# A recurrent layer's input projection, moved from a stage of its own into the steps of the recurrence

## The chip, the core and the metric

One NeuronCore of a Trainium2 chip runs the whole kernel. The metric is device time in microseconds (us); lower is better. The engines are named as in the profile: PE is TensorE (PEld its weight loads), DVE is VectorE, ACT is ScalarE, POOL is GpSimd, SP is SyncE, which here only issues DMAs. A "q" behind an engine's name (SPq, DVEq) means its sequencer, which issues, waits and computes registers.

## The reference, cut to what matters

The model is a GRU over 512 time steps, followed by differential attention, a Fourier filter, a second attention and a mixture of experts. Only the GRU is touched. With B = 4 sequences, T = 512 steps and D = 512 features, everything in float32:

```python
def cell(h, x):
    gi = x @ W_ih + b_ih          # input part: depends on no state
    gh = h @ W_hh + b_hh          # recurrent part: needs the last step's h
    i_r, i_z, i_n = jnp.split(gi, 3, axis=-1)
    h_r, h_z, h_n = jnp.split(gh, 3, axis=-1)
    r = jax.nn.sigmoid(i_r + h_r)
    z = jax.nn.sigmoid(i_z + h_z)
    n = jnp.tanh(i_n + r * h_n)
    h_new = (1.0 - z) * n + z * h
    return (h_new, h_new)
```

The input part of all steps can be computed at any time before its step; the recurrent part is a chain of 512 links.

## The kernel before

Features lie on the 128 partitions in KD = 4 chunks. Engines are programmed by hand, each with its own instruction list, and meet only in counting semaphores: `wait_ge(sem, n)` holds an engine's list until the semaphore has reached n. Nothing is reordered between waits.

`gate_inputs_stage` (L55) forms the input part for all steps at once. It loads x and W_ih, transposes x on PE (L118) into `xT`, and DVE copies the transposes out of PSUM (L173) and spreads the weight columns (`spread_w`, L175). Then, for the r and n gates, 4 sequences x 8 column chunks x 4 contraction chunks give 128 matmuls with 512 moving columns each (L127); ACT (L167) and DVE (L200) take turns moving the results, with bias, to `giT`. Then 16 blocks of the z gate's input follow (L147), which DVE adds to its bias (L205) in `giz`.

`gru_stage` (L208) runs the 512 steps. In a step, PE issues four small matmuls that add the z input through a selection matrix (`add_z_input`, L294), four that add the n bias (`add_bias`, L288), and then 16 matmuls for each of r, n and z (`gate`, L303), whose stationary operand is the state `h`. Four matmuls at a time run side by side, on four column groups of the array. DVE transposes the r rows (L364), adds `giT` (L366), transposes n and z rows (L368, L377), and forms the new state in two scans (L384), one for a quarter of it and one for the rest. After them it keeps the state in `hsT` (L388). ACT makes the sigmoids and the tanh. POOL copies a selection column (`pick`, L279) two steps ahead, and once in 32 steps a block of z inputs (`zin`, L274). SP loads the next stage's weights and clears two DRAM buffers (16 MB) beside the first steps.

The matmuls of `add_z_input` and `add_bias` for step s stand ahead of `step(s)` in PE's list, so they run in the tail of step s-1, while DVE and ACT finish the state.

Of the kernel before, what the change touches and what calls it, by code (L numbers as in the profile page):

```python
# [7 lines left out]
F32 = mybir.dt.float32  # L8
# [3 lines left out]
ALU = mybir.AluOpType  # L12
# [3 lines left out]
P = 128  # L16
B, T, D = 4, 512, 512
KD = D // P
# [36 lines left out]
def gate_inputs_stage(nc, t, x, W_ih, b_ih, b_hh, h0, W_hh):  # L55
# [3 lines left out]

    with ExitStack() as ctx:  # L60
# [4 lines left out]
        xT = t.wide[:].rearrange("p (b k t) -> p b k t", b=B, k=KD)  # L65
        bias = ctx.enter_context(nc.sbuf_tensor("gi_bias", [P, 2, GC], F32))
# [7 lines left out]
        gi_psum, gi_even, gi_odd = sem("gi_psum"), sem("gi_even"), sem("gi_odd")  # L74
        z_psum, z_out = sem("z_psum"), sem("z_out")
# [5 lines left out]
        def _(sp):  # L81
# [4 lines left out]
            sp.wait_ge(w_in[KD - 1], 16)  # L86
# [24 lines left out]
        def _(pe):  # L111
# [9 lines left out]
            def gate(b, c):  # L121
                m = b * NG + c
                if m >= 4:
                    pe.wait_ge(gi_even if c % 2 == 0 else gi_odd, (m - 4) // 2 + 1)
                col = GATES[c // KD] * D + (c % KD) * P
                for k in range(KD):
                    last = nc.tensor.matmul(pg[:, c % 4, :], wih[:, k, col:col + P], xT[:, b, k, :], start=(k == 0), stop=(k == KD - 1))  # L127
                last.then_inc(gi_psum, 1)

            pe.wait_ge(ident_in, 16)  # L130
            for k in range(KD):
                transpose_x(0, k)
            pe.wait_ge(w_spread, 3 * KD)
# [6 lines left out]
            pe.wait_ge(gi_even, B * NG // 2)  # L140
            pe.wait_ge(gi_odd, B * NG // 2)
            for kb in range(T // 32):
                if kb >= 4:
                    pe.wait_ge(z_out, kb - 3)
                for k in range(KD):
                    for b in range(B):
                        last = nc.tensor.matmul(pg[32 * b:32 * b + 32, kb % 4, :], xT[:, b, k, 32 * kb:32 * kb + 32], wih[:, k, D:2 * D],  # L147
                                                start=(k == 0), stop=(k == KD - 1))
                last.then_inc(z_psum, 1)

        def gate_input(b, c):
            return t.giT[:, :, b + c * B], pg[:, c % 4, :], GATES[c // KD] * KD + c % KD

        @block.scalar
        def _(act):
            for n, bvec in enumerate((b_ih, b_hh)):
                for j in range(KD):
                    for g in GATES:
                        act.dma_start(bias[32 * j:32 * j + 32, n, g * KD:(g + 1) * KD],
# [3 lines left out]
            for b in range(B):  # L163
                for c in range(0, NG, 2):
                    to, of, g = gate_input(b, c)
                    act.wait_ge(gi_psum, b * NG + c + 1)
                    nc.scalar.activation(to, of, ACT.Identity, bias=bias[:, 0, g:g + 1]).then_inc(gi_even, 1)  # L167

        @block.vector
        def _(dve):  # L170
            def copy_x(b, k):
                dve.wait_ge(xT_psum, b * KD + k + 1)
                nc.vector.tensor_copy(xT[:, b, k, :], pt[:, k % 2, :]).then_inc(xT_ready, 1)  # L173

            def spread_w(k):  # L175
                dve.wait_ge(w_in[k], 16)
                for g in range(3):
                    dst, src = wih[:, k, g * D:(g + 1) * D], wraw[:, k, g * D:(g + 1) * D]
# [6 lines left out]
            for k in range(KD):  # L185
                copy_x(0, k)
            for k in range(KD):
                spread_w(k)
# [4 lines left out]
            dve.wait_ge(bias_ready, 1)  # L193
            dve.wait_ge(zbias_ready, 1)
            for b in range(B):
                for c in range(NG):
                    if c % 2:
                        to, of, g = gate_input(b, c)
                        dve.wait_ge(gi_psum, b * NG + c + 1)
                        nc.vector.tensor_scalar(to, of, bias[:, 0, g:g + 1], None, ALU.add).then_inc(gi_odd, 1)  # L200
                    if b < B - 1 and c in (3, 4, 5, 6):
                        copy_x(b + 1, c - 3)
            for kb in range(T // 32):
                dve.wait_ge(z_psum, kb + 1)
                nc.vector.tensor_tensor(t.giz[:, kb, :], pg[:, kb % 4, :], zbias[:, 0, :], ALU.add).then_inc(z_out, 1)  # L205


def gru_stage(nc, t, b_hh, next_weights):  # L208

# [5 lines left out]
    with ExitStack() as ctx:  # L215
# [5 lines left out]
        whh = t.ahead[:].rearrange("p (c g j f) -> p c g j f", c=KD, g=3, j=KD)  # L221
        bias, one = sb("bias", [P, KD, P]), sb("one", [P, 8 * B])
# [7 lines left out]
        pz = ctx.enter_context(nc.psum_tensor("gru_pz", [P, 2, 4 * P], F32))  # L230
        zero_set, cleared = sem("zero_set"), sem("cleared")
# [15 lines left out]
        def _(sp):  # L247
# [3 lines left out]
            sp.wait_ge(h_ready, 2)  # L251
            w = t.ahead2[:].rearrange("p (n c f) -> p n c f", n=3, c=KD)
            for n, W in enumerate(next_weights):
                for jj in range(KD):
                    sp.dma_start(w[32 * jj:32 * jj + 32, n, :, :],
                                 W.rearrange("(jj c i) n -> jj i c n", jj=KD, c=KD)[jj]).then_inc(ahead_in, 16)
# [1991 lines left out]
```

## Time and profile before

| | |
|---|---|
| median of 3 runs | 4371.38 us (4367.14 to 4373.53) |
| profiled execution, own time | 4358.2 us |
| its span in the trace | 4356.4 us |
| input stage, until the last z block | about 194 us |
| the 512 steps | from 199 us to about 2067 us |
| everything behind the GRU | about 2289 us |
| PE busy over the span | 3723.3 us (85%) |

All rows come from the profiled execution. A row's time counts from the span's start. "Busy" of PE counts a matmul up to its modelled end, which overlaps the next one's start, so the distance from start to start says more than the duration. Matmuls in float32 show as two records each, one for each of their two passes.

### The profile page before, as it was taken

To read this page: it belongs to the slowest core of one execution; us is meant where nothing else is said; L and a number is where in the kernel's file an instruction comes from. 1 tells how busy PE (TensorE), PEld (TensorE's weight loads), DVE (VectorE), ACT (ScalarE), POOL (GpSimd) and SP (SyncE) were. 2 spreads that over 40 slices of the span, in tenths; PEclk is the share of its full clock that TensorE was granted. 3 is DMA by queue.
4 is the path that set the end of the run, shared out by engine and by line. 5 is a ranking of instruction groups with operands and counts; after the bars stand their busy time and mean duration, and the time that the engine had idled before them with its cause. 6 is when DMAs were issued, how large, how long until landed. Compare 5 with 4: busy or idle time off the path is not lost. (4 is left out here: it accounts for less than half of the span.)

```text
span 4356.4 us, 166845 instructions
## 1 busy us (share of the span) xinstructions
PE 3723.3 (85%) x68264; PEld 2388.6 (55%) x68325; DVE 2283.1 (52%) x6296; ACT 1383.6 (32%) x4235; POOL 524.3 (12%) x1081
## 2 busy tenths in 40 slices
PE   8988888888888888888899999688999989688840
PEld 4477777777777777777344444243333344344420
DVE  2255555555555555555577777435666633222234
ACT  1133333333333333333344444223444411111100
POOL 0000000000000000000122222000000024200036
PEclk9999999999999999999999999799999989899975
DMA  3130000000000000000211110101121112288868
GB/s 102 42 142 0 0 0 0 0 0 0 0 0 0 0 0 0 0 0 0 68 52 34 51 51 17 71 29 52 51 67 51 52 59 83 86 261 257 262 197 191
DMA packets 136991, 253.11 MB, mean 58 GB/s; under 512 B 22136, under 2 KB 69380, under 8 KB 135013
## 3 DMA queue, kind: packets, MB, share of 16 engines
q1 hardware_dynamic: 97188, 157.86, 11.1%
q0 software_dynamic: 21056, 52.52, 4.5%
q10 hardware_dynamic: 18688, 41.96, 3.2%
q8 instruction: 36, 0.59, 0.1%
q14 instruction: 23, 0.18, 0.0%
HBM read 147.89 MB, written 62.92 MB: 48 GB/s over the span
## 5 line engine op out<-in xcount | busy, mean ns | idle before, releaser
L303 PE MATMUL gru_pr<-ahead,h 128*4 128x128 f32 x16384 | 556.6, 274 | 193.5 <-DVE h L384 193.5
L303 PEld LDWEIGHTS gru_pr<-ahead,h 128*4 128x4 f32 x16384 | 338.7, 87 | 399.3 <-DVE h L384 330.6
L303 PE MATMUL gru_pn<-ahead,h 128*32 128x128 f32 x16384 | 541.0, 273 | 0.0
L303 PE MATMUL gru_pz<-ahead,h 128*4 128x128 f32 x16384 | 540.9, 273 | 0.0
L303 PEld LDWEIGHTS gru_pn<-ahead,h 128*32 128x32 f32 x16384 | 457.9, 110 | 1.3
L303 PEld LDWEIGHTS gru_pz<-ahead,h 128*4 128x4 f32 x16384 | 437.4, 87 | 8.5
L331 ACT ACTIVATE gru_rn<-gru_pre 128x16 f32<-128x16 f32 x512 | 119.5, 233 | 704.5 <-DVE gru_pre L366 704.5
L364 DVE STREAM_TRANSPOSE gru_tr<-gru_pr 128x128 f32<-128x128 f32 x512 | 162.1, 317 | 335.3 <-PE gru_pr L303 335.3
L279 POOL COPY gru_pick<-ident 128x4 f32 x512 | 95.9, 187 | 1649.3 <-PE gru_pz L294 1644.0
L890 DVE TENSOR_REDUCE da_mx<-da_ps 128x2 f32<-128x1024 f32 (+3 forms) x256 | 201.1, 816 | 132.9 <-PE da_ps L580 132.9
L377 DVE STREAM_TRANSPOSE gru_tz<-gru_pz 128x32 f32<-128x32 f32 (+1 forms) x1024 | 195.0, 229 | 118.4 <-PE gru_pz L303 118.4
L384 DVE TENSOR_TENSOR_SCAN h<-gru_d 128x16 f32<-128x16 f32 (+1 forms) x1024 | 226.2, 228 | 57.2
L336 ACT ACTIVATE gru_d<-gru_tz 128x4 f32<-128x4 f32 (+1 forms) x1024 | 198.1, 216 | 109.2 <-DVE gru_tz L377 109.2
L797 ACT ACTIVATE da_probT<-da_ps 128x1024 f32<-128x1024 f32 (+3 forms) x256 | 169.5, 701 | 196.5 <-PE da_ps L601 196.5
L368 DVE STREAM_TRANSPOSE gru_tn<-gru_pn 128x128 f32<-128x128 f32 x512 | 162.2, 317 | 119.1 <-PE gru_pn L303 119.1
L333 ACT ACTIVATE gru_d<-gru_narg 128x32 f32<-128x32 f32 x512 | 120.2, 235 | 328.1 <-DVE gru_narg L373 328.1
L294 PE MATMUL gru_pz<-gru_zin,gru_pick 128*4 128x128 f32 x4096 | 205.8, 273 | 5.4 <-DVEq L357 5.4
L288 PE MATMUL gru_pn<-gru_bias,gru_one 128*32 128x128 f32 x4096 | 205.8, 273 | 0.0
L1790 POOL DMA_INDIRECT xg<-ro_yb,ro_slot x96 | 93.9, 978 | 898.8 <-issue 825.3
L507 POOL TENSOR_SCALAR_AFFINE_SELECT da_probT<-da_probT 128x256 f32<-128x256 f32 x256 | 142.1, 566 | 421.9 <-ACT da_probT L797 421.9
L1979 PE MATMUL ex_pg<-ahead,ex_xT 128*128 128x384 f32 x512 | 191.1, 520 | 0.0
L1574 DVE TENSOR_REDUCE fa_mx<-fa_ps 128x2 f32<-128x1024 f32 x128 | 150.4, 1216 | 44.9 <-PE fa_ps L1393 44.8
(283 smaller groups left out, 5419.9 us busy)
## 6 DMA issues: line engine op xcount, KB each, us to landing
ahead<-in_L_ffn_gate_up_proj SPq DMA_DIRECT2D x64, 768.0 KB, 4.9
ex_wd<-in_L_ffn_down_proj ACTq DMA_DIRECT2D x64, 384.0 KB, 6.2
xg<-gru_zeros SPq DMA_DIRECT2D x4, 4096.0 KB
ex_xg<-xg ACTq DMA_DIRECT2D x64, 256.0 KB, 5.7
eo<-ex_eo POOLq DMA_DIRECT2D x64, 256.0 KB, 5.2
ahead<-wide SPq DMA_DIRECT2D x15, 1024.0 KB, 4.7
ahead<-xnT SPq DMA_DIRECT2D x15, 1024.0 KB
da_wg<-ahead SPq DMA_DIRECT2D x45, 256.0 KB, 4.8
```

Source lines behind the costliest of these rows:

```text
L288: nc.tensor.matmul(pn[32 * j:32 * j + 32, 0:P], one[:], bias[:, j, :], start=True, stop=False)
L294: last = nc.tensor.matmul(pz[32 * j:32 * j + B, par, 0:P], pick[:, par, :], zin[:, j * P:(j + 1) * P], start=True, stop=False)
L303: last = nc.tensor.matmul(rows(j), of(c), whh[:, c, g, j, :], start=(c == 0 and start), stop=(c == KD - 1))
L336: nc.scalar.activation(cb(d1[:, part.start * B:part.stop * B, 2]), tz[:, part, 0:B], ACT.Sigmoid).then_inc(z_act, 1)
L364: nc.vector.transpose(tr[:].rearrange("p c x -> p (c x)"), pr[:, 0:P]).then_inc(tr_done, 1)
L368: nc.vector.transpose(tn[:], pn[:, 0:P]).then_inc(tn_done, 1)
L377: nc.vector.transpose(tz[:, part, :].rearrange("p c x -> p (c x)"), pz[:, par, part.start * 32:part.stop * 32]).then_inc(tz_done, 1)
L384: nc.vector.tensor_tensor_scan(t.h[:].rearrange("p c x -> p (c x)")[:, part.start * 32:part.stop * 32:2], d0[:, of, :].rearrange("p c o -> ...
L797: nc.scalar.activation(probT[:, n % 2, 2 * part:2 * part + 2, n * P:T], ps[:, KBANK[2 * part]:KBANK[2 * part] + 2, n * P:T], ACT.Exp, scal ...
L890: nc.vector.tensor_reduce(mx[:, i, a, 2 * part:2 * part + 2], ps[:, bank:bank + 2, 0:(i + 1) * P], AX, ALU.max).then_inc(max_done, 1)
L1574: nc.vector.tensor_reduce(mx[:, i, 2 * half:2 * half + 2], ps[:, 2 * half:2 * half + 2, :], AX, ALU.max).then_inc(max_done, 1)
L1979: last = nc.tensor.matmul(pg[:, u % 2, 0:2 * I], xT[:, u % 2, k, :], wg[:, u, k, :], start=(k == 0), stop=(k == KD - 1))
```

## The change

In the input stage the r and n inputs are formed for the first 32 steps only: 8 x 4 matmuls with 128 moving columns (4 sequences x 32 steps). All of x is transposed first; the load of x[1] no longer waits for W_ih. The z part is as before, with two PSUM buffers in place of four. `xT` is laid out with the chunk outermost.

The other 15 blocks of 32 steps are formed within the steps of the block ahead, one column chunk c of 8 in four steps. In step 4c+k PE issues one more matmul, of contraction chunk k, into a new PSUM tile `pgi`, between `add_bias` and `step` (`next_gate_input`). Its stationary operand is `wst`, one SBUF buffer into which POOL copies the four 128x128 weight blocks of column chunk c, ahead of the pick of the third step. After the fourth step DVE moves `pgi` with its bias to `giT` (`move_gate_input`). The semaphore `gi_out` starts at 1 and counts these moves. The weights W_ih stay in `ahead2` until the last block, so the loads of the next stage's weights go behind the clearing and behind the last of these matmuls in SP's list.

```diff
@@ gate_inputs_stage
-            sp.wait_ge(w_in[KD - 1], 16)
             sp.dma_start(xin[:, 1, :, :], x[1]...).then_inc(x_in[1], 16)
...
-            for b in range(B):
-                pe.wait_ge(xT_ready, (b + 1) * KD)
-                for c in range(NG):
-                    gate(b, c)
-                    if b < B - 1 and c in (3, 4, 5, 6):
-                        transpose_x(b + 1, c - 3)
+            for b in range(B):
+                for k in range(KD):
+                    transpose_x(b, k)
+            pe.wait_ge(w_spread, 3 * KD)
+            pe.wait_ge(xT_ready, B * KD)
+            for c in range(NG):
+                if c >= 2:
+                    pe.wait_ge(gi_out, c - 1)
+                for k in range(KD):
+                    last = nc.tensor.matmul(pg[:, c % 2, 0:B * 32], wih[:, k, c * P:(c + 1) * P], xT[:, k, :, 0:32], start=(k == 0), stop=(k == KD - 1))
+                last.then_inc(gi_psum, 1)
@@ gru_stage, gpsimd
+            with pool.Fori(0, NBL - 1) as kb:
+                block_of_z(kb)
+                with pool.Fori(0, NG) as c:
+                    for k in range(KD):
+                        if k == 2:
+                            pool.wait_ge(gi_out, kb * NG + c + 1)
+                            nc.gpsimd.tensor_copy(wst[:], wih[:, :, bass.ds(c * P, P)]).then_inc(wst_ready, 1)
+                        pick_step(kb, c * KD + k, k)
@@ gru_stage, tensor
+            def next_gate_input(kb, c, k):
+                if k == 0:
+                    pe.wait_ge(gi_out, kb * NG + c + 1)
+                    pe.wait_ge(wst_ready, kb * NG + c + 1)
+                last = nc.tensor.matmul(pgi[:, 0:P], wst[:, k, :], xT[:, k, :, bass.ds(kb * 32 + 32, 32)],
+                                        start=(k == 0), stop=(k == KD - 1))
+                if k == KD - 1:
+                    last.then_inc(gi_psum, 1)
...
+                    for k in range(KD):
+                        s = kb * 32 + c * KD + k
+                        add_z_input(s, k % 2)
+                        add_bias(s)
+                        next_gate_input(kb, c, k)
+                        step(s, k % 2)
@@ gru_stage, vector
+            def move_gate_input(kb, c):
+                dve.wait_ge(gi_psum, kb * NG + c + 1)
+                nc.vector.tensor_tensor(t.giT[:, bass.ds(kb * 32 + 32, 32), bass.ds(c * B, B)], pgi[:, 0:P].rearrange("p (b t) -> p t b", b=B),
+                                        t.gi_bias[:, 0, bass.ds(c, 1)].unsqueeze(2).broadcast_to([P, 32, B]), ALU.add).then_inc(gi_out, 1)
+            with dve.Fori(0, NBL - 1) as kb:
+                with dve.Fori(0, NG) as c:
+                    for k in range(KD):
+                        if k == 0:
+                            dve.wait_ge(gi_out, kb * NG + 1)
+                        step(kb * 32 + c * KD + k, k % 2)
+                    move_gate_input(kb, c)
```

How the lists stand now. In the rows below a wait shows the name under which a semaphore was first made; `gi_x_in1` is `gi_out` here, `gi_x_in0` is `gi_psum`, and `gi_w_in0` is `wst_ready`. PE's list for the first of four steps, from the z input to the r gate, before:

```order
L292 ISA [waits gi_zb_in]
L294 MATMUL gru_pz<-gru_zin,gru_pick 4x128 [waits gru_tz_done]
L294 MATMUL gru_pz<-gru_zin,gru_pick 4x128 x3
L288 MATMUL gru_pn<-gru_bias,gru_one 32x128 [waits gi_gi_psum]
L288 MATMUL gru_pn<-gru_bias,gru_one 32x128 x3
L301 REGISTER_ALU
L303 MATMUL gru_pr<-ahead,h 4x128 [waits gi_w_in2]
```

and after the change:

```order
L289 MATMUL gru_pn<-gru_bias,gru_one 32x128 x3
L316 ISA
L318 ISA [waits gi_w_in0,gi_x_in1]
L318 MATMUL gru_pgi<-wide,gru_wst 128x128
L302 REGISTER_ALU
L304 MATMUL gru_pr<-ahead,h 4x128 [waits gi_ident_in]
```

The new matmul and its two waits stand ahead of the r gate's first matmul. On DVE, the end of the fourth step after the change, with the move behind the copy of the state:

```order
L408 SCALAR_TENSOR_TENSOR h<-gru_d 128x48 [waits gru_z_act]
L411 REGISTER_ALU
L412 ISA [waits gi_ident_in]
L412 COPY wide<-h 128x16
L415 ISA
L416 ISA [waits gi_x_in0]
L416 TENSOR_TENSOR giT<-gru_pgi,gi_bias 128x32x4
```

Before the change a loop's branch followed the copy. On POOL, the third step's part of the list after the change:

```order
L267 COPY gru_pick<-ident 128x4
L274 ISA
L275 ISA [waits gi_x_in1]
L275 COPY gru_wst<-ahead 128x512
L266 ISA [waits gi_whh_in]
L267 ISA [waits gi_xT_ready]
L267 COPY gru_pick<-ident 128x4
```

Before the change only picks stood there. The copy waits for `gi_out`, the count of DVE's moves.

## Rows read from the trace of the kernel before

**Rows 1.** The profile's page: span and instructions.

```profile
span 4356.4 us, 166845 instructions
```

**Rows 2.** Windows: stretch, length, busy of PE PEld DVE ACT POOL, PEclk, DMA, GB/s.

```profile
0.00:19.66 19.66, 3.50 (x16) 2.78 (x16) 6.75 (x18) 0.00 (x0) 2.54 (x8) 0.95 0.79 260
19.66:138.68 119.02, 117.76 (x304) 54.21 (x305) 25.48 (x30) 19.62 (x17) 0.00 (x0) 0.98 0.21 51
138.68:194.60 55.92, 55.14 (x512) 20.00 (x512) 11.05 (x16) 0.00 (x0) 0.00 (x0) 1.00 0.00 1
194.60:2067.50 1872.90, 1674.76 (x57344) 1445.06 (x57344) 1081.25 (x4616) 665.57 (x3071) 106.08 (x529) 1.00 0.03 11
```

**Rows 3.** The timeline where one step ends: start, us, engine, line, what, [idle before].

```profile
1002.26 0.40 PE L294 MATMUL gru_pz<-gru_zin,gru_pick 128*4 128x128 f32 x8
1002.48 0.40 PE L288 MATMUL gru_pn<-gru_bias,gru_one 128*32 128x128 f32 x8
1003.00 0.43 DVE L384 TENSOR_TENSOR_SCAN h<-gru_d 128x16 f32<-128x16 f32 x2
1003.25 1.08 PE L303 MATMUL gru_pr<-ahead,h 128*4 128x128 f32 x32 [0.37 <-DVE h L384]
1003.57 0.19 DVE L388 COPY wide<-h 128x16 f32 x1
1004.40 0.32 DVE L364 STREAM_TRANSPOSE gru_tr<-gru_pr 128x128 f32<-128x128 f32 x1 [0.65 <-PE gru_pr L303]
```

**Rows 4.** Who waited for whom, PE in the GRU: us, times, longest.

```profile
PE gru_pr L303 <- DVE h L384: 193.5, 511, 0.7
```

**Rows 5.** The timeline where a new block of z inputs is copied.

```profile
312.76 0.40 PE L294 MATMUL gru_pz<-gru_zin,gru_pick 128*4 128x128 f32 x8
313.36 0.61 POOL L274 COPY gru_zin<-giz 128x512 f32 x1 [7.09 <-PE gru_pz L294]
313.50 0.67 DVE L384 TENSOR_TENSOR_SCAN h<-gru_d 128x16 f32<-128x16 f32 x2
314.07 1.06 PE L303 MATMUL gru_pr<-ahead,h 128*4 128x128 f32 x32 [0.69 <-DVE h L384]
314.27 0.41 POOL L279 COPY gru_pick<-ident 128x4 f32 x2 [0.30 <-POOL gru_zin L274]
```

**Rows 6.** Groups by line in the input stage: shapes, count | busy us, mean ns.

```profile
L127 PE MATMUL gi_pg<-wide,ahead 128*128 128x512 f32 x256 | 114.5, 603 | 4.9 <-DVE ahead L182 4.9
L200 DVE TENSOR_SCALAR giT<-gi_pg,gi_bias 128x512 f32<-128x512 f32 x16 | 17.6, 1100 | 77.3 <-PE gi_pg L127 77.3
L173 DVE COPY wide<-gi_pt 128x512 f32<-128x512 f32 x16 | 10.9, 685 | 29.0 <-PE gi_pt L118 29.0
```

**Rows 7.** Groups of the new matmul's shape elsewhere in the kernel, back to back.

```profile
L562 PE MATMUL da_ps<-da_wg,ahead 128*128 128x128 f32 x480 | 61.6, 281 | 0.0
L562 PEld LDWEIGHTS da_ps<-da_wg,ahead 128*128 128x128 f32 x480 | 55.8, 191 | 6.8 <-issue 5.0
```

**Rows 8.** The timeline of the first 20 us: first transposes, and SP's load of x[1].

```profile
11.21 3.52 PE L118 MATMUL gi_pt<-ident,gi_xin 128*128 128x128 f32 x16 [11.21 <-DMA gi_xin<-in_x]
17.13 0.38 SPq L87 DMA_DIRECT2D gi_xin<-in_x  x1
```

**Rows 9.** The GRU's first gate: timeline, and windows over it.

```profile
200.05 1.93 PE L303 MATMUL gru_pr<-ahead,h 128*4 128x128 f32 x32
202.05 0.32 DVE L364 STREAM_TRANSPOSE gru_tr<-gru_pr 128x128 f32<-128x128 f32 x1 [2.59 <-PE gru_pr L303]
...
199.20:201.90 2.70, 2.65 (x52) 2.05 (x56) 0.18 (x1) 0.47 (x2) 0.19 (x1) 0.50 0.53 150
```

**Rows 10.** First and last of 19 PE gaps of 1.7 to 2.7 us; one window.

```profile
2094.53 0.93 PE L577 MATMUL da_ps<-da_kp,da_q 32*128 32x384 f32 x8 [2.34 <-DVE da_mx L890]
4138.94 0.74 PE L1971 MATMUL ex_px<-ident,ex_xg 128*128 128x128 f32 x4 [2.09 <-DMA ex_wd<-in_L_ffn_down_proj]
...
2751.70:2755.00 3.30, 2.80 (x16) 0.52 (x8) 0.72 (x1) 0.38 (x1) 0.00 (x0) 0.50 0.00 0
```

More of the change, by code:

```diff
@@ L64, in gate_inputs_stage @@
         xin = ctx.enter_context(nc.sbuf_tensor("gi_xin", [P, 2, TT, D], F32))
[L65 to L66 removed]
+        xT = t.wide[:].rearrange("p (k b t) -> p k b t", b=B, k=KD)
+        bias = t.gi_bias
         zbias = ctx.enter_context(nc.sbuf_tensor("gi_zbias", [P, 2, D], F32))
@@ L157, in _ @@
                 for j in range(KD):
-                    for g in GATES:
-                        act.dma_start(bias[32 * j:32 * j + 32, n, g * KD:(g + 1) * KD],
+                    for m, g in enumerate(GATES):
+                        act.dma_start(bias[32 * j:32 * j + 32, n, m * KD:(m + 1) * KD],
                                      bvec.rearrange("(g j c i) -> g j i c", g=3, j=KD, c=KD)[g, j],
@@ L162, in _ @@
             act.wait_ge(bias_ready, 1)
[L163 to L167, printed above, removed]
+            for c in range(NG):
+                act.wait_ge(gi_psum, c + 1)
+                nc.scalar.activation(t.giT[:, 0:32, c * B:(c + 1) * B], pg[:, c % 2, 0:B * 32].rearrange("p (b t) -> p t b", b=B),
+                                     ACT.Identity, bias=bias[:, 0, c:c + 1]).then_inc(gi_out, 1)
         @block.vector
@@ L183, in spread_w @@
                                               src.rearrange("p (j c i) -> p c j i", c=KD, j=KD)).then_inc(w_spread, 1)
[L185 to L188, printed above, removed]
+            for b in range(B):
+                for k in range(KD):
+                    copy_x(b, k)
+                    if b == 0:
+                        spread_w(k)
             dve.wait_ge(b_in, 16 * (4 * KD))
@@ L192, in _ @@
             nc.vector.tensor_tensor(zbias[:, 0, :], zbias[:, 0, :], zbias[:, 1, :], ALU.add).then_inc(zbias_ready, 1)
-            dve.wait_ge(bias_ready, 1)
             dve.wait_ge(zbias_ready, 1)
[L195 to L202, printed above, removed]
             for kb in range(T // 32):
                 dve.wait_ge(z_psum, kb + 1)
-                nc.vector.tensor_tensor(t.giz[:, kb, :], pg[:, kb % 4, :], zbias[:, 0, :], ALU.add).then_inc(z_out, 1)
+                nc.vector.tensor_tensor(t.giz[:, kb, :], pg[:, 2 + kb % 2, :], zbias[:, 0, :], ALU.add).then_inc(z_out, 1)
 def gru_stage(nc, t, b_hh, next_weights):
@@ L230, in gru_stage @@
         pz = ctx.enter_context(nc.psum_tensor("gru_pz", [P, 2, 4 * P], F32))
+        pgi = ctx.enter_context(nc.psum_tensor("gru_pgi", [P, 4 * P], F32))
+        wst = sb("wst", [P, KD, P])
+        gi_psum, gi_out, wst_ready = sem("gi_psum"), sem("gi_out"), sem("wst_ready")
         zero_set, cleared = sem("zero_set"), sem("cleared")
@@ L262, in _ @@
             sp.dma_start(t.eo_dram[SLOTS:SLOTS + 1, :], zeros[0:1, 0, :]).then_inc(cleared, 16)
+            sp.wait_ge(cleared, 16 * (SLOTS // (R * P) + 1))
+            sp.wait_ge(gi_psum, (NBL - 1) * NG)
+            w = t.ahead2[:].rearrange("p (n c f) -> p n c f", n=3, c=KD)
+            for n, W in enumerate(next_weights):
+                for jj in range(KD):
+                    sp.dma_start(w[32 * jj:32 * jj + 32, n, :, :],
+                                 W.rearrange("(jj c i) n -> jj i c n", jj=KD, c=KD)[jj]).then_inc(ahead_in, 16)
             sp.wait_ge(ahead_in, 16 * 3 * KD)
-            sp.wait_ge(cleared, 16 * (SLOTS // (R * P) + 1))
         @block.gpsimd
@@ L323, in _, with step @@
             act.wait_ge(set_up, 6)
-            with act.Fori(0, T) as s:
+            def step(s, kb):
                 gi = t.giT[:, bass.ds(s, 1), :].rearrange("p o c -> p (o c)")
+                act.wait_ge(gi_out, kb * NG + 1)
                 nc.scalar.activation(rn[:, :, 3], gi[:, ST:2 * ST], ACT.Copy).then_inc(gin_ready, 1)
@@ L336, in _ @@
                     nc.scalar.activation(cb(d1[:, part.start * B:part.stop * B, 2]), tz[:, part, 0:B], ACT.Sigmoid).then_inc(z_act, 1)
+            with act.Fori(0, NBL) as kb:
+                with act.Fori(0, 32) as n:
+                    step(kb * 32 + n, kb)
         @block.vector
@@ L357, in _ @@
             dve.sem_inc(tz_done, 4)
+            dve.sem_inc(gi_out, 1)
             nc.vector.tensor_copy(state, t.hin[:].rearrange("p c b -> p (c b)")).then_inc(h_ready, 2)
```

61 lines of the change are left out of this document (26 added, 35 removed).

## The prediction, on record before the changed kernel ran

> **What bounds the kernel now.** I read the stages first, then one step. By the windows [rows 2] the input stage has PE busy nearly throughout: 117.76 of 119.02 us for the r and n inputs, 55.14 of 55.92 us for z. The steps take the stretch from 194.6 to 2067.5 us. They are a chain, and the timeline of one step [rows 3] shows its tail. Call T the start of an r gate (1003.25). PE started the z input at 1002.26 and the bias at 1002.48. Groups of four start 0.22 us apart, so the bias has streamed by about T-0.55, and PE then has nothing until the first scan delivers a quarter of the state. The trace books 0.37 us of idle time there, in all 193.5 us over 511 steps [rows 4]. Behind T, DVE still has its second scan and the copy of the state, which starts at T+0.32 and ends at T+0.51. It then sits idle until the r rows are ready at T+1.15. So each step has two holes: about 0.55 us on PE ahead of T, and 0.65 us on DVE from T+0.5. The next r gate comes about 3.64 us after the last (511 steps in 1868 us, less the block boundaries).
>
> **What the change removes.** The r and n inputs of all steps were 128 matmuls at 512 columns, 114.5 us with the transposes of later x between them [rows 2, 6]. Now there are 32 matmuls at 128 columns. The same shape back to back takes 61.6 us for 480 records, 0.257 us per matmul of two records [rows 7]: 8.2 us, and some 2 us more for a start at the low clock. In front of them all of x must now be transposed. The first x is transposed at 11.2 us, and W_ih is in at 17.1 us, because SP's load of x[1] waited for exactly that [rows 8]. With x[1] (1 MB) in the same traffic at 260 GB/s [rows 2] both are in by about 21 us. x[2] can go once x[0]'s buffer is free (about 15 us), x[3] once x[1] is transposed (about 23 us). A load of 1 MB takes 4 us at that rate and about 2 us to begin, so x[3] is there at 29 us, and four copies of 0.685 us [rows 6] end at about 32 us. The z part then begins at 32 + 10 = 42 us, where it now begins at 138.7 us: **-96 us**, between -90 (loads later by 7 us) and -104 (loads just hidden). Its own 55 us stay. W_hh still follows x[3] in SP's queue and has that long to land.
>
> **What it adds in three steps of four.** One matmul with 128 columns, 0.257 us, goes into PE's hole of 0.55 us. It ends at about T-0.3: nothing. If the hole were filled, the price would be up to 0.26 us x 360 = 94 us; at half clock it is filled. ACT's extra wait on `gi_out` is for a move made a step earlier. SP's later weight loads (3 MB) go out at step 480 with 32 steps left, over 110 us: nothing.
>
> **What it adds in the fourth step.** Here the order of the lists decides. At k = 0 PE waits, ahead of the r gate, for `gi_out` >= 8kb+c+1. The semaphore starts at 1, so this wants all 8kb+c earlier moves done, the move of chunk c-1 among them. That move stands behind the state copy of the step that has just produced h. And `wst_ready` wants POOL's copy of chunk c, which waits for that same move. So move, copy and matmul run one after another, at a time when h is ready and nothing else can run; queued behind the waiting matmul are the r, n and z gates, and behind these DVE and ACT. The waits of PE and POOL would be harmless if they looked one chunk back; with a single `wst` and `pgi` they don't. From the rows, after T (where the r gate would start):
>
> - The move can start once the copy of the state is over (T+0.51) and two register instructions are through: T+0.60.
> - Its duration is not in the trace. It reads 128x128 from PSUM and writes with a stride. Below it lies nothing shorter than the 0.19 us copy of 16 elements; above it the 128x512 move with strided write, 1.10 us [rows 6]. The nearest row is the 128x128 transpose from PSUM, 0.32 us [rows 3]. I take 0.35: T+0.95.
> - DVE to POOL: I take the 0.20 us that lay between a z input's end (312.97 + 0.19 of drain) and POOL's copy at 313.36 [rows 5]: T+1.15.
> - POOL's copy of 128x512 float32: 0.61 us, the same size as `zin` [rows 5]: T+1.76.
> - POOL to PE: between 0.05 (scan to r gate) and 0.30 (copy to pick, [rows 5]). I take 0.15: T+1.91.
> - Weight load 0.19 and two passes of 0.12 [rows 7], now exposed: 0.43, so T+2.34.
>
> A stall of 2.34 us, 119 times (the first chunk of the first block finds `gi_out` at 1): **+278 us**. The ends are 1.7 us (203 us) with the shortest of each, and 3.4 us (401 us) with the longest.
>
> On the copy's duration the Trainium skill has a figure of its own: its page GPSIMD Engine Reference (section 3.1, Elementwise) gives 768 ns, measured and predicted, for 512 elements in a tight loop. By it the sum would be an estimated 19 us higher (0.16 x 119). This case's row has 0.61 us, and I use the row.
>
> The place of the copy matters too. Where POOL's 0.61 us copy ran beside the scans, these took 0.67 us in place of 0.43, and PE's wait grew from 0.37 to 0.69 us [rows 3, 5]. The new copy runs from T+1.15 to T+1.76, when the scans are over and DVE's next work waits for PE, so I count nothing; beside the scans it would cost 0.3 x 120 = 36 us. The page SBUF — State Buffer of the Trainium skill (section Who interferes with whom) has the rule for it: a DVE instruction with two SBUF inputs contends with a GpSimd instruction that reads SBUF. The trace agrees, with its 0.24 us on two scans.
>
> **The clock.** During the stall PE is idle from T-0.55 to T+1.9, about 2.45 us, 119 times. The steps run at 1.00 of the clock [rows 2]. Elsewhere in this trace there are 19 PE gaps of 1.7 to 2.7 us at full clock; 15 of them are followed by a stretch at 0.50 (1.2 in place of 2.4 GHz), such as that from 2751.7 us [rows 10]. What it costs here shows at the GRU's start, at 0.50: r gate to transpose takes 2.00 us in place of 1.15 [rows 3, 9], 0.85 us a gate, so 0.85 to 1.7 us when one or two gates lie in it. With 15 of 19 gaps and 1.7 us this would be 160 us; with none, nothing. The steps around my gaps are denser (89% busy, [rows 2]) than the attention and expert stages where those 19 lie, so I take two falls in five gaps, 48 at 1.25 us: **+60 us**.
>
> **Sum.** The profiled execution took 4358.2 us, its span is 4356.4 [rows 1]. 4358 - 96 + 278 + 60 = 4600. The median of the runs lies 13 us above the profiled one, so the forecast for a median is **4610 us**, 5.5% above before.
>
> **Rivals.**
> - *The stall alone, no fall of the clock.* For it: 1.00 through 1870 us of steps, and 4 of the 19 gaps kept the clock. 4358 - 96 + 278 + 13 = 4553 us. Chance 0.20.
> - *The clock falls at nearly every stall.* For it: 15 of 19. 4553 + 160 = 4713 us. Chance 0.15.
> - *Not slower.* The stall costs nothing where it's under 96/119 = 0.81 us. It would have to be hidden, by the move running ahead of the scans, or the copy ahead of the move. Then 4371 - 96 = 4275 us. Against it: the move alone can't end before T+0.7, the copy takes 0.61 us, and both are ordered by the wait. It holds only if I have miscounted the waits by one chunk. Chance 0.05.
> - *A shorter chain*, 1.7 to 2.0 us, without clock loss: 4371 - 96 + 203 to 238 = 4478 to 4513. Chance 0.05.
>
> The forecast itself (stall, and clock falls at some of the stalls) has 0.55 and reaches from 4565 to 4670.
>
> **How the numbers follow.** The range takes in the forecast, most of the case without falls, and the case of falls at nearly all: 4520 to 4725. Left out are the shorter chain, the not slower case and the long ends. A change of 0.2% (9 us) is about what a measurement of this kernel can tell. Every case but one lies more than 2% above, so slower has 0.95, faster 0.04 (nearly all of "not slower"), same 0.01.
>
> **What would show it.** Right: z input (L137) starting near 42 us; the r gate's first matmul after every fourth step idle for over 2 us, with the releaser of the L318 matmul being POOL's `wst` copy, in all 119 times and 240 to 330 us with clock losses; POOL copies of 0.61 us; steps between stalls still 3.64 us; PEclk below 1.00 in the 40 slices of the steps. Wrong: `wst` copies that lie ahead of the scans' end, or PE idle time ahead of L318 of under 0.8 us; steps of 3.9 us throughout would mean that the matmul doesn't fit its hole.

## The result, and the profile after

The changed kernel takes 4597.07 us (median of 4 runs, 4592.65 to 4597.49), the kernel before 4372.45 us (4 runs beside it, 4367.14 to 4379.56). The ratio is 1.0517, with a 95% interval from 1.0501 to 1.0532: the change makes the kernel 5.2% slower. The profiled execution took 4597.14 us. First lines of its page, which answer to [rows 1]: span, then PE's two rows, then the granted clock in 40 slices.

```profile
span 4595.5 us, 169709 instructions
PE 3856.7 (84%) x69093; PEld 2527.4 (55%) x69093; DVE 2303.1 (50%) x6400; ACT 1317.6 (29%) x4227; POOL 589.9 (13%) x1201
PEclk9999999999999999999999999989999989899975
```

**The input stage gets shorter, as meant.** The timeline of its first 43 us (start, us, engine or queue, line, what, [idle before, releaser]):

```profile
2.88 1.01 SPq L86 DMA_DIRECT2D gi_xin<-in_x  x1
3.93 16.92 SPq L89 DMA_DIRECT2D hin<-in_cond  x16
20.44 3.93 PE L117 MATMUL gi_pt<-ident,gi_xin 128*128 128x128 f32 x16 [4.54 <-DMA gi_xin<-in_x]
20.89 3.89 SPq L94 DMA_DIRECT2D gi_xin<-in_x  x2
26.57 6.70 PE L117 MATMUL gi_pt<-ident,gi_xin 128*128 128x128 f32 x28 [2.20 <-DMA gi_xin<-in_x]
37.87 5.62 PE L130 MATMUL gi_pg<-wide,ahead 128*128 128x128 f32 x48 [0.91 <-ACT giT L152]
43.42 55.14 PE L137 MATMUL gi_pg<-ahead,wide 128*32 128x512 f32 x512
```

The z part begins at 43.42 us, where it began at 138.68 [rows 2]: 95.3 us earlier, with its own 55.14 us as before. What holds it there is x. SyncE issues the load of x[2] at 20.89 us, behind its 16 small transfers, and that of x[3] at 24.40 us, when the last transposes of x[1], whose buffer it takes, have gone out. The r and n matmuls follow the last copy of x.

**The steps pay it back three times over.** The same place in two steps of the changed kernel, first k = 3 to k = 0, then an ordinary one. T, where the r gate would start, is 0.245 us behind the first scan, as in [rows 3]: 1004.86.

```profile
1004.61 0.44 DVE L408 TENSOR_TENSOR_SCAN h<-gru_d 128x16 f32<-128x16 f32 x2
1005.18 0.19 DVE L412 COPY wide<-h 128x16 f32 x1
1005.53 0.29 DVE L416 TENSOR_TENSOR giT<-gru_pgi,gi_bias 128x128 f32 x1 [0.17 <-issue]
1005.99 0.61 POOL L275 COPY gru_wst<-ahead 128x512 f32 x1 [4.99 <-DVE giT L416]
1006.84 0.30 PEld L318 LDWEIGHTS gru_pgi<-wide,gru_wst 128*128 128x128 f32 x2 [2.61 <-issue]
1006.85 0.48 PE L318 MATMUL gru_pgi<-wide,gru_wst 128*128 x2 [2.35 <-POOL gru_wst L275]
1007.26 1.06 PE L304 MATMUL gru_pr<-ahead,h 128*4 128x128 f32 x32
1008.39 0.32 DVE L388 STREAM_TRANSPOSE gru_tr<-gru_pr 128x128 f32<-128x128 f32 x1 [2.56 <-PE gru_pr L304]
...
1010.44 0.49 PE L318 MATMUL gru_pgi<-wide,gru_wst 128*128 x2
1010.63 0.44 DVE L408 TENSOR_TENSOR_SCAN h<-gru_d 128x16 f32<-128x16 f32 x2
1010.88 1.09 PE L304 MATMUL gru_pr<-ahead,h 128*4 128x128 f32 x32
```

Read it as a relay: copy of the state, move, copy of the weight block, matmul, and only then the r gate, at T+2.40. In the ordinary step the matmul has run before the scans deliver, and the r gate follows the first scan by 0.25 us. The waits from 90 to 2250 us (us in total, times, longest) count how often:

```profile
POOL gru_wst L275 <- DVE giT L416: 583.9, 119, 7.4
PE gru_pgi L318 <- POOL gru_wst L275: 273.1, 119, 2.4
PE gru_pr L304 <- DVE h L408: 10.5, 35, 0.4
```

The wait of [rows 4] for the scan (193.5 us in 511 steps) has all but gone: the new matmul and its waits lie in its place. DVE's first and last transpose of the 512 steps bound the recurrence:

```profile
107.73 0.32 DVE L388 STREAM_TRANSPOSE gru_tr<-gru_pr 128x128 f32<-128x128 f32 x1 [3.44 <-PE gru_pr L304]
...
2291.01 0.32 DVE L388 STREAM_TRANSPOSE gru_tr<-gru_pr 128x128 f32<-128x128 f32 x1 [0.65 <-PE gru_pr L304]
```

That is 2183.3 us, where the kernel before took 1863.8 (202.05, in [rows 9], to 2065.89). From such starts I take three numbers for each kernel below: this total; the median distance of steps that don't cross from k = 3 to k = 0, and of those that do. Before they are 3.639 and 3.639; after 3.641 and 6.020.

### The profile page after: what moved, and what is told of

It is laid out like the page before. It is cut to its first block and busy times, and to the rows that moved or that the text cites. A ratio compares the mean times of both kernels' runs of the same rounds, so it can differ in the third digit from the quotient of the medians.

```text
span 4595.5 us, 169709 instructions
## 1 busy us (share of the span) xinstructions
PE 3856.7 (84%) x69093; PEld 2527.4 (55%) x69093; DVE 2303.1 (50%) x6400; ACT 1317.6 (29%) x4227; POOL 589.9 (13%) x1201
## 5 line engine op out<-in xcount | busy, mean ns | idle before, releaser
L318 PE MATMUL gru_pgi<-wide,gru_wst 128*128 x960 | 237.8, 330 | 273.2 <-POOL gru_wst L275 273.1
L304 PEld LDWEIGHTS gru_pr<-ahead,h 128*4 128x4 f32 x16384 | 354.9, 88 | 147.3 <-DVE h L408 27.1
L318 PEld LDWEIGHTS gru_pgi<-wide,gru_wst 128*128 128x128 f32 x960 | 145.4, 191 | 376.6 <-issue 376.6
```

The source lines that it names most:

```text
L304: last = nc.tensor.matmul(rows(j), of(c), whh[:, c, g, j, :], start=(c == 0 and start), stop=(c == KD - 1))
L318: last = nc.tensor.matmul(pgi[:, 0:P], wst[:, k, :], xT[:, k, :, bass.ds(kb * 32 + 32, 32)], start=(k == 0), stop=(k == KD - 1))
```

## The experiments

Nine kernels ran, in three groups (e1 to e4, e5 to e7, e8 and e9); each group shares its runs of the kernel before. All start from the changed kernel. A kernel is called slower or faster when its whole interval lies over 2% away from before: the changed kernel, e4, e6 and e9 are slower, e8 is the same, and e1, e2, e3, e5 and e7 stay open at that bound, since their intervals take in 0.98 or 1.02.

| kernel | median us | before, us | ratio, interval | 512 steps | k=0..2 | k=3 to 0 |
|---|---|---|---|---|---|---|
| changed | 4597.07 | 4372.45 | 1.0517, 1.0501 to 1.0532 | 2183.3 | 3.641 | 6.020 |
| e1_move_early | 4301.65 | 4382.35 | 0.9823, 0.9798 to 0.9848 | 1883.9 | 3.639 | 3.639 |
| e2_copy_early | 4473.25 | 4382.35 | 1.0213, 1.0181 to 1.0245 | 2054.7 | 3.639 | 5.137 |
| e3_no_next_inputs | 4285.32 | 4382.35 | 0.9798, 0.9770 to 0.9826 | 1870.8 | 3.639 | 3.639 |
| e4_pe_filled | 4573.27 | 4382.35 | 1.0451, 1.0425 to 1.0478 | 2158.8 | 3.640 | 6.021 |
| e5_transfers_later | 4264.19 | 4350.13 | 0.9803, 0.9788 to 0.9818 | 1870.3 | 3.639 | 3.639 |
| e6_two_banks | 4574.04 | 4350.13 | 1.0511, 1.0488 to 1.0534 | 2192.8 | 3.640 | see text |
| e7_x_first | 4263.86 | 4350.13 | 0.9798, 0.9778 to 0.9818 | 1870.3 | 3.639 | 3.638 |
| e8_banks_in_loop | 4292.90 | 4348.78 | 0.9887, 0.9857 to 0.9918 | 1908.6 | 3.638 | 3.958 |
| e9_loop_of_8 | 4556.21 | 4348.78 | 1.0491, 1.0464 to 1.0519 | 2177.5 | 3.639 | see text |

### e1_move_early: the move ahead of the step

```diff
                     for k in range(KD):
                         if k == 0:
                             dve.wait_ge(gi_out, kb * NG + 1)
+                        if k == 3:
+                            move_gate_input(kb, c)
                         step(kb * 32 + c * KD + k, k % 2)
-                    move_gate_input(kb, c)
```

> The changed kernel with one call moved: DVE makes the move of a chunk ahead of its fourth step's work instead of behind it. All instructions, buffers and waits are the same. Theory (the serial chain move, copy, matmul makes the loss): the move falls into DVE's idle 0.65 us ahead of the r rows, the copy runs a step earlier, and PE finds both waits met. Then the 119 stalls of 2.38 us go, 283 us, and with them the low clock, and the time is 4372 - 95 = 4277, plus some 15 us of slow first passes: 4280 to 4300 us, under the kernel before. First rival (the added work itself costs the time: matmuls that don't fit the hole, clock, longer loops): it stays above 4500 us. Second rival (GpSimd's copy, now beside DVE's scans or additions, slows them by 0.3 us): 36 us more than the theory, 4315 to 4335 us.

Measured 4301.65 us, 0.982 of before and below both kernels, by intervals that lie clear of each other. It is 2 us over the theory's range; the kernel before took 4382 us in this group, where the theory had started from 4372. The stall is gone from every step, and with it 299 of the 319.5 us by which the recurrence had grown. The timeline of one such step:

```profile
1002.73 0.18 DVE L412 COPY wide<-h 128x16 f32 x1
1003.09 0.29 DVE L416 TENSOR_TENSOR giT<-gru_pgi,gi_bias 128x128 f32 x1 [0.17 <-issue]
1003.55 0.61 POOL L275 COPY gru_wst<-ahead 128x512 f32 x1 [1.35 <-DVE giT L416]
1003.57 0.32 DVE L388 STREAM_TRANSPOSE gru_tr<-gru_pr 128x128 f32<-128x128 f32 x1 [0.18 <-PE gru_pr L304]
```

Move and copy now start a whole step before TensorE wants them, and the move fits DVE's hole: the transpose behind it still waits 0.18 us for TensorE, where it waited 0.65 [rows 3].

### e2_copy_early: the copy off the chain, the move still on it

```diff
-                            pool.wait_ge(gi_out, kb * NG + c + 1)
+                            pool.wait_ge(gi_psum, kb * NG + c + 1)
```

(`gi_psum` starts at 1 instead of 0, and its other waits are one higher. The copy then waits only for the matmul that has last read `wst`.)

> The changed kernel with the copy alone taken out of the chain: GpSimd's copy waits for the last matmul of the chunk ahead (gi_psum, which now starts at 1) and no longer for DVE's move; the move stays behind the fourth step. Theory of a serial chain: copy and its hand-over (0.61 + about 0.25 us) leave the stall, so 119 x 0.86 = 102 us less than the changed kernel, 4495 us; but the copy now runs at the time of the scans of the third step's end, and if it slows them as the z block's copy did, 0.3 us come back 120 times, 36 us: 4531 us. Rival (the stall is not made of these pieces, for instance PE's own restart after a long idle time): the time stays within 20 us of 4597.

Measured 4473.25 us. The step from k = 3 to k = 0 takes 5.137 us, 0.88 less than in the changed kernel. TensorE's waits now name the move:

```profile
PE gru_pgi L318 <- DVE giT L417: 166.4, 118, 1.5
```

So the stall of 2.38 us has two parts: 1.50 us of move and its two handovers with the matmul, 0.88 us of copy and handover (0.61 of it the copy's own time). The rival, that the stall is not made of these pieces, fell. The copy did not slow the scans either: it starts 0.2 us behind the r gate, when they are over, and meets the copy of the state instead. The time came out 22 us under the expectation of 4495, mainly since fewer stretches of low clock are left: 3 in the steps in place of 17, none of them at a stall.

### e3_no_next_inputs: the loops alone

All calls of `next_gate_input` and `move_gate_input`, POOL's copies and their waits are taken out, and zeros set once. This kernel leaves out the r and n inputs of blocks 1 to 15, and its time is that of the steps without the added work.

> The changed kernel without the r and n inputs of blocks 1 to 15: no matmuls, copies and moves within the steps; zeros stand in their place. The loops of four steps are kept. It prices the input stage and the loops alone. Theory: 95 us less than the kernel before, plus the slow first passes, if they belong to the loop and not to the added work: 4277 to 4295 us. Against the first experiment it tells what the hidden work still costs: theory under 10 us. Rival (the hidden work is not free): this one is 30 us or more under the first experiment.

Measured 4285.32 us, 16 us under e1 in the same group, with intervals that overlap; the steps of the trace differ by 13.1 us. That lies between the theory (under 10) and the rival (30 or more). The step medians are those of e1, so the matmul, the move and the copy are hidden in the 3.64 us of a step when they are placed as in e1. The 13.1 us lie in two places. Steps 480 and 481 take 9.22 and 5.00 us in e1 and 3.64 and 3.67 here: 6.9 us. And 14 steps at the turn of a block (31, 63 and so on) take 4.02 to 4.07 us in e1 and 3.64 here: 5.6 us. At such a turn TensorE's z input starts 1.93 us behind the transpose of the r rows in place of 1.50, in both kernels. Without the new matmul the r gate still follows the scan by 0.25 us; with it, by 0.66. So there the matmul no longer fits the hole. Steps 0 to 2 are slow here too (4.48, 4.47 and 7.88 us), without any of the added work.

### e4_pe_filled: TensorE kept busy in the stall

```diff
                 if k == 0:
+                    for _ in range(8):
+                        nc.tensor.matmul(pfill[:, 0:P], t.ident[:], bias[:, 0, :], start=True, stop=True)
                     pe.wait_ge(gi_out, kb * NG + c + 1)
```

> The changed kernel with eight useless 128x128 matmuls on PE ahead of the two waits, into a PSUM bank that nobody reads; they last 2.06 us and lie in the stall of 2.4 us. Theory: the chain of waits is unchanged, and only the falls of the clock go: the trace shows 17 low stretches in the steps, each costing about 1.1 us, so 15 to 25 us less than the changed kernel, 4572 to 4582 us. Rival (PE's restart, not the chain, makes the stall, or the useless matmuls delay the useful one): no gain, or a loss of up to 0.1 us x 119 = 12 us, 4597 to 4609 us.

Measured 4573.27 us. The stalls are as long as before (6.021 us), and in the steps one stretch at a granted clock of 0.50 is left of 17. The windows over the steps of both kernels, changed first (columns as in [rows 2]):

```profile
107.70:2291.00 2183.30, 1883.56 (x58201) 1612.41 (x58197) 1113.53 (x4719) 613.45 (x3066) 170.07 (x643) 0.99 0.02 8
```

```profile
109.00:2269.00 2160.00, 2094.39 (x60146) 1820.91 (x60142) 1114.15 (x4722) 613.97 (x3067) 170.01 (x643) 1.00 0.02 8
```

The recurrence is 24.5 us shorter. 20.0 of these lie at the falls to 1.2 GHz: 13 of the 17 began at or just behind a stall. In ten of them the stalled step took 7.15 us in place of 6.02 and the one behind it 0.38 more on average, 1.5 us together; in the other three the step behind took 5.26 in place of 3.64. Another 5.2 us come from steps 480 and 481, which took 7.40 and 5.04 us in the changed kernel and take 3.58 and 3.64 here (see e5). So the useless matmuls buy back 20 us of clock, and the rest is not shown to be the clock's.

### e5_transfers_later: SyncE's bulk transfers away from the loops' first passes

In e1 five steps remained slow: 4.27, 4.86 and 8.63 us for steps 0 to 2, and 9.22 and 5.00 us for 480 and 481, the first through TensorE's second loop. In them TensorE waits for no semaphore, as here in step 2 of the changed kernel, while the DMA engines are full (share 1.04 in the window below):

```profile
117.66 0.83 PE L304 MATMUL gru_pz<-ahead,h 128*4 128x128 f32 x23
121.99 0.81 PE L304 MATMUL gru_pz<-ahead,h 128*4 128x128 f32 x9 [3.50 <-issue]
...
104.00:130.00 26.00, 20.42 (x472) 15.36 (x472) 8.37 (x36) 4.77 (x24) 1.34 (x5) 0.80 1.04 382
```

The edit, on top of e1's:

```diff
             sp.wait_ge(zero_set, 1)
+            sp.wait_ge(hs_kept, 32)
...
             sp.wait_ge(gi_psum, (NBL - 1) * NG)
+            sp.wait_ge(hs_kept, T - 24)
```

> As e1_move_early, but SyncE issues the clearing of xg only after 32 steps are kept, and the three weight arrays of the next stage only 24 steps before the end. In e1 four steps are slow with TensorE idle for no semaphore (steps 0 to 2 took 4.27, 4.86 and 8.63 us, steps 480 and 481 took 9.22 and 5.00, against 3.64), each the first pass through one of its loops, and both times SyncE's bulk transfers fill the DMA engines. Theory: TensorE's instructions come late because their transfer queues behind the bulk ones; with these moved, the five steps take about 3.64 to 4 us, the 512 steps 1870 us in place of 1883.9, and the time is some 13 us less than e1's, 4285 to 4292. Rival: a first pass is slow by itself; then the steps stay at 4.3 to 9.2 us, and the time at 4298 to 4304.

Measured 4264.19 us, 0.9803 of before. In microseconds it lies under the theory's range, but so does the kernel before in this group (4350 us in place of 4382). The five steps take 4.29, 3.64, 3.64, 3.64 and 3.64 us, and the recurrence 1870.3 us, 13.6 less than in e1; but for the first step's 4.29, that is the theory's. The same place as above, in step 2 of e5:

```profile
115.68 1.06 PE L306 MATMUL gru_pz<-ahead,h 128*4 128x128 f32 x32
116.56 0.40 PE L297 MATMUL gru_pz<-gru_zin,gru_pick 128*4 128x128 f32 x8
```

No record names what was waited for. What speaks for the theory is the time of the packets on the queue that carries instructions. In e1 the weights' transfers ran from 1867.4 to 1882.4 us, and two instruction packets went within them, 4.1 and 10.0 us behind the r transpose of step 480. In e5 the same two went 1.0 us ahead of that transpose and 2.5 us behind it, with no transfer beside them. But bulk transfers alone don't make a first pass slow. In e4 the weights' transfers lay over steps 480 and 481 as in e1, with one instruction packet among them in place of two, and the steps took 3.58 and 3.64 us. The kernel before, whose loop on TensorE holds two steps, ran its first five in 3.64 to 3.69 us beside the same clearing and weights. The ratio alone would not tell e5 from e1, since the intervals overlap; the steps do. Against the kernel before, the recurrence is 6.5 us longer, 5.5 of them the turns of the blocks, as in e1.

### e6_two_banks: the product in two banks in turn

`pgi` gets a second PSUM bank, used for odd c; TensorE waits for the move before the last instead of the last, POOL's copy for the matmul as in e2, and the move stays behind the step. To have the bank fixed in the code, TensorE's and VectorE's loops were written out for 8 steps:

```diff
-                with pe.Fori(0, NG) as c:
-                    for k in range(KD):
+                with pe.Fori(0, NG // 2) as cc:
+                    for m in range(2 * KD):
...
-                        next_gate_input(kb, c, k)
+                        next_gate_input(kb, cc * 2 + m // KD, m % KD, m // KD)
```

> The changed kernel with the move left behind the step, as it was, but the product in two PSUM banks in turn, and the copy of the weight block waiting for the last matmul that reads the old one; TensorE's and VectorE's loops hold 8 steps in place of 4. Theory: the stall is TensorE's wait for the move and for the copy, so with neither on its way the step from k = 3 to k = 0 takes 3.64 us again in place of 6.02, and the time is within 15 us of e1's 4302. Rival: moving the move early is what mattered (the move itself, 0.29 us behind the state's copy, holds VectorE up): then that step takes 3.9 to 4.1 us, and the time is 4335 to 4360. Of the slow first passes: if they come with the length of TensorE's loop, there are about twice as many slow steps, up to step 7, and 13 us more; if they come from the bulk transfers alone, the same sum as in e1, some 13 to 15 us.

Measured 4574.04 us, over 200 us above both expectations. The stall itself is gone: inside the body, from its fourth to its fifth step, the distance is 3.638 us with the move left where it was. But at each turn of the loop TensorE idles anew (8.2 us for that step, the median of 60):

```profile
1012.18 1.06 PE L304 MATMUL gru_pz<-ahead,h 128*4 128x128 f32 x32
1016.65 0.40 PE L295 MATMUL gru_pz<-gru_zin,gru_pick 128*4 128x128 f32 x8 [3.41 <-issue]
1017.61 1.69 PE L304 MATMUL gru_pr<-ahead,h 128*4 128x128 f32 x32
...
q8 instruction: 573, 9.39, 0.8%
```

The last row is that of the queue that carries instructions: 573 packets and 9.39 MB; in e5's page it reads:

```profile
q8 instruction: 38, 0.62, 0.1%
```

The 535 more are about 9 for each turn of the 60 passes. The first pass, beside the bulk transfers, was slow in all of its steps 0 to 6 (4.3 to 8.6 us), 16 us over 3.64 in all, where e1 had 7 us in steps 0 to 3. That is in line with the expectation for a longer loop. Two changes were mixed in this kernel, so two more took them apart.

### e9_loop_of_8: only the longer body

e5 with the two lines of the loop above written out for 8 steps on TensorE, and nothing else.

> As e5_transfers_later, with TensorE's loop written out for 8 steps in place of 4 and nothing else: the same instructions in the same order, and every wait the same. Theory: the instruction queue carries some 570 packets in place of 38, TensorE idles 3.4 to 4 us at each of the 60 turns and runs the next passes at the lower clock level, as in e6 (8.1 us in place of 3.64 at the turn, and 0.45 more in the step behind it): the 512 steps take 1870 + 60 x 4.9 = 2160 us, and the time is about 290 us over e5's, 1.046 of before. Rival: e6's loss is of the two banks or of VectorE's longer loop; then this one is as e5, 0.980 of before.

Measured 4556.21 us, 1.0491 of before: the same instructions in the same order, with the same waits, cost 0.069 of the time more than in e5, which is 299 us; the recurrence is 307 us longer, where 290 were expected. In its page and its waits:

```profile
q8 instruction: 573, 9.39, 0.8%
...
PE gru_pz L297 <- issue: 192.9, 60, 3.9
```

So TensorE fetches a body of 8 steps again at each turn, and not one of 4. The rival fell: neither the two banks nor VectorE's loop is needed for the loss. In the first pass, with the bulk transfers later, steps 1 to 6 take 3.64 us each.

The Trainium skill, on its page Runtime: NRT & Kernel Launch (section Instruction fetch mechanics), has TensorE's instruction memory at 128 KiB, refilled in blocks of 16 KiB by a DMA queue that its sequencer drives. The trace agrees in the size of a block: the packets are of 16.4 KB, and 9 of them, about 147 KB and so more than 128 KiB, go into each turn. The same section says that a taken branch whose target lies outside the current window of 2 pages stalls. A stall there is at each turn of the long body; but the body of 4 steps, an estimated 74 KB (half of 147) and so more than 2 pages, was kept, and on this the measurement differs. The section also has the crossing of a 16 KiB boundary mostly hidden; in e1's first passes, with the DMA engines full, it was not.

### e8_banks_in_loop: two banks with the short body

As e6, but the bank is the variable of a loop of its own around 4 steps, and the transfers are as in e5.

```diff
-                with pe.Fori(0, NG) as c:
+                with pe.Fori(0, KD) as cc, pe.Fori(0, 2) as bank:
...
-        last = nc.tensor.matmul(pgi[:, 0:P], ...
+        last = nc.tensor.matmul(pgi[:, bass.ds(bank * 4 * P, P)], ...
```

> As e6_two_banks (move behind the step, product in two banks in turn, copy early), but the bank is chosen by a loop of its own around a body of 4 steps, and SyncE's bulk transfers are later, as in e5_transfers_later. In e6 the step from the fourth to the fifth in the body took 3.638 us with the move left behind it; what made e6 slow was about 3.4 us of TensorE idle once in each body of 8 steps, for no semaphore, with 573 packets on the instruction queue in place of 38. Theory: that is TensorE fetching a body that it can't keep, and with 4 steps in it the step from k = 3 to k = 0 takes 3.64 us every time, the instruction queue has about 38 packets, and the time is e5's, 0.980 of before. Rival: an outer loop's turn costs something too, or the move behind the step does at a loop's end; then some of the steps from k = 3 to k = 0 take 4 us or more, and the time is over 0.985 of before.

Measured 4292.90 us, 0.9887. The instruction queue is back at 38 packets, and the stall doesn't return, so neither the place of the move nor the copy's length had to be slow in itself. But part of the rival holds too: the step at the turn of the inner loop is 0.28 us longer and that at the turn of the outer 0.59, of which the next step gives back 0.17 and 0.02. That makes 60 x (0.28 + 0.59 - 0.19) = 41 us; the recurrence is 38.3 us longer than e5's. At the outer turn TensorE's z input comes 0.61 us late, with all that it waits for long done, and the r gate with it. At the inner turn it comes 0.15 us late, and the other half of the 0.28 is VectorE's, whose transpose of the r rows follows the r gate 0.15 us later than elsewhere; the next step makes that up. In e5 the turn of a loop of 4 steps costs nothing (3.64 us), so it isn't the turn as such. Whether the further level, the bank's address or the move at the turn makes it was not tried.

### e7_x_first: SyncE's small transfers behind x

e5 with the loop of 16 `hin` transfers below the loads of x[2] and x[3] in SyncE's list.

> As e5_transfers_later, and the 16 small transfers of hin, whose issues took SyncE 16.92 us in the changed kernel's trace, stand behind the loads of x[2] and x[3]. Theory: those loads waited for SyncE's queue, x[2] from about 16.3 us (last transpose of x[0]) to 20.89, and x[3] follows; the z part then starts at 39 to 41 us in place of 43.4, and the time is 2 to 5 us under e5's, which the trace can tell and the time hardly. Rival: the loads are held by the DMA engines, not by the queue, and the start stays at 43 us.

Measured 4263.86 us beside e5's 4264.19. The z part starts at 42.19 us in place of 42.83, 0.64 us earlier and not 2 to 4. SyncE issued the two loads from 14.76 us on instead of 20.78, yet the transposes of x[3] began only at 29.11 instead of 30.72. Six us of head start in the queue gave 1.6 us at the data, so the rival's time is nearer, though for another reason. The head start is x[2]'s alone. The load of x[3] was issued at 24.04 us here and at 24.29 in e5, both times just behind the transposes of x[1], whose buffer it takes; and these began when x[1] had come, at 20.08 and 20.33 us. In the queue x[3] had nothing to gain.

## Why the prediction was right

It forecast 4610 us, with a likeliest case of 4565 to 4670; measured 4597.07. In the traces 239.1 us were added (a span of 4595.5 less 4356.4), to rounding: -94.3 until the first transpose, +319.5 within the steps, +14.0 behind them (2304.5 against 2290.5 us).

- **Input stage, -96 us:** measured -95.3. The start was forecast at 42 us and is 43.42. Two parts of its working were off and nearly cancelled: the last copy of x ended at 34.8 us in place of 32, and the r and n matmuls began the z part 8.6 us behind it in place of 10. The `hin` transfers, whose issues hold SyncE's queue for 16.92 us, were not counted; they held x[2], but e7 prices them at 0.6 us only. The order that the prediction had for x[3], behind the transposes of x[1], is the one that held.
- **The matmul in TensorE's hole, 0 in three steps of four:** right. Those steps take 3.641 us, as before 3.639.
- **The stall, 2.34 us x 119 = 278 us:** the mechanism, the count and the releaser are right. It measures 2.38 us (6.020 less 3.639), 283 us in all. Link by link: the move starts at T+0.67 (0.60), lasts 0.29 us (0.35); the copy starts at T+1.13 (1.15) and lasts 0.61 (0.61); the weight load starts at T+1.98 (1.91), since POOL's handover to TensorE is 0.24 us where I took 0.15; r gate at T+2.40 (2.34). All 120 copies took 0.61 us. The 768 ns that the Trainium skill gives for 512 elements (GPSIMD Engine Reference, section 3.1, Elementwise) did not show.
- **Contention of the copy, 0:** right. Where it was moved beside other DVE work (e2, e6, e8) it did cost something, out of the path (below).
- **The clock, 48 falls at 1.25 us = 60 us:** this is the term that was mis-sized. There were 17 stretches at 0.50 in the steps, 13 of them at one of the 119 stalls and 4 at the first step or behind slow first passes, and e4 puts the price of the 13 at 20 us. A fall at a stall costs some 1.5 us, near the 1.25 taken; it was their number that was wrong, 13 in place of 48. The share of the 19 gaps of [rows 10] in other stages did not carry over, and no run shows why.
- **Not forecast:** slow first passes of TensorE's loops, 13.6 us by e1 against e5, and 15.4 us in steps 0 to 4, 480 and 481 of the changed kernel. Its steps sum up as 283 (stall) + 20 (clock) + 15.5 (first passes) + 1 (the rest) = 319.5 us.
- **Behind the steps,** 14 us more in the trace stand in no term. The routing stage alone, from its first to its last instruction on a tile of its own (`ro_...`), took 275.0 us in place of 253.5. Its code is unchanged, and it took 274.7 to 278.4 us in e1 to e4 and 249.0 to 249.5 in e5 to e9. In e6, where nothing behind the recurrence and nothing in SyncE's order differs from the changed kernel, it took 249.2, so it does not go with the change. It goes with the group of runs, as the times of the kernel before do (4382, 4350 and 4349 us). Why was not tried.

**The rivals.** The case of falls at nearly every stall (4713 us) and the shorter chain (4478 to 4513) are out. The stall without falls (4553) is e4's case, to 20 us. What the rival "not slower" asked for, the move ahead of the scans, is e1's edit, a whole step ahead, and it gives 4302 us.

By the prediction's own working, 60 us of clock stood where 20 of clock, 16.5 of first passes and the rest, and 14 behind the steps were measured, 50.5 in all. That the total was good to 13 us is in part luck: what it left out made up for what it set too high.

The gain that the change was after is real, and e1 collects it: 95 us of input stage, of which the first passes take 14 and the turns of the blocks 6. With these first passes mended (e5) the kernel is at 0.980 of before, the fastest version with the full result here, level with e7.

## What to carry to other kernels

Work that is tucked into a recurrent loop is hidden only if every link of its chain is done before its reader wants it. Look for the one instruction that stands behind the loop's last product in its engine's list: moving one call up by one step was worth 299 us here. Check the hole at the turns as well as inside the loop: at the blocks' turns it was too short, and each cost 0.4 us. When a wait looks back to the latest use of a single buffer, either start its chain earlier or give it a second buffer, but count what the second buffer does to the loop's body and turns. And a loop on TensorE has a size at which it stops being free, here between 4 and 8 steps: compare the packets of the instruction queue before and after unrolling.

## What the runs showed of the hardware

- **A loop body is kept or fetched again.** With 4 steps in TensorE's loop the instruction queue carried 38 packets; with 8 steps 573, and TensorE idled 3.2 us on average in 60 waits for no semaphore (192.9 us), mostly followed by a stretch of low clock; in all 307 us (e9 against e5).
- **First passes were slow beside bulk transfers.** They took up to 9.2 us a step in place of 3.64 in e1, and 3.64 but for a first step of 4.29 in e5, with the transfers moved. By the packets' times their instructions came late. It takes more than the transfers: steps 480 and 481 of e4 and the first steps of the kernel before ran at 3.58 to 3.69 us beside them.
- **The turn of an outer loop can show on the path.** TensorE's first matmul behind it came 0.43 us later at the blocks' turns (e1, e3, e5) and 0.61 us later at the outer turn of e8; at the turn of the plain loop of 4 steps in e5, 0.01 us.
- **POOL's copy beside a DVE copy.** With the two at the same time, DVE's copy of the state took 0.55 us in place of 0.18, out of the path, in 105 steps of e8. Its timeline:

```profile
1001.48 0.61 POOL L277 COPY gru_wst<-ahead 128x512 f32 x1 [0.43 <-PE gru_pgi L320]
1001.58 0.55 DVE L415 COPY wide<-h 128x16 f32 x1
```

- **Gaps of 2.35 us did not always bring the clock down:** in the changed kernel it fell at 13 of 119, one in nine, to 0.50 for 3.4 us each.
